# Sorting tokens to experts in a hybrid transformer kernel: where the rows are written, when, and in runs of how many

## The reference, cut to what matters

```
probs = softmax(t @ w_gate); tw, ti = top_k(probs, 2); tw = tw / sum(tw)
for e in range(8):
    we = sum(where(ti == e, tw, 0))
    h = gelu(t @ w1[e] + b1[e]) @ w2[e] + b2[e]      # 128 -> 512 -> 128
    out = out + we * h
```

## Time and profile before

| what | us |
|---|---|
| three runs | 902.31, 901.24, 893.77 (median 901.24) |
| the profiled execution, own time | 898.2 |
| its span, first to last instruction | 896.4 |
| PE busy | 767.0 (86%) |
| DVE, ACT, POOL busy | 544.5, 543.4, 484.2 |
| mean granted TensorE clock | 0.923 |

### The profile page before, as it was taken

How to read it: one execution, slowest core, us unless ns; L and a number is a source line. 1 busy time by engine, 2 the same in 40 slices (tenths; PEclk the granted TensorE clock), 3 DMA queues, 4 the chain that set the end, 5 groups by cost and what they waited for, 6 DMA issues and landing times.

```text
span 896.4 us, 21301 instructions
## 1 busy us (share of the span) xinstructions
PE 767.0 (86%) x7166; PEld 546.7 (61%) x7166; DVE 544.5 (61%) x1370; ACT 543.4 (61%) x1264; POOL 484.2 (54%) x906
## 2 busy tenths in 40 slices
PE   1999999999999399697988999999999948968970
PEld 1756655666565189497964565566666525958970
DVE  4699899788988123012486887878889822211232
ACT  0377777878787256154546676787877834715640
POOL 6667678747762621504645665844777273060436
PEclk9999999999999789698999899999999977978995
DMA  9300000000000436266210000000000042635842
GB/s 274 111 3 3 3 2 3 4 3 3 4 2 4 130 107 175 79 182 175 79 38 13 16 18 5 4 3 3 3 3 3 3 124 77 173 103 143 245 124 67
DMA packets 57657, 56.29 MB, mean 63 GB/s; under 512 B 6856, under 2 KB 42448, under 8 KB 57552
## 3 DMA queue, kind: packets, MB, share of 16 engines
q1 hardware_dynamic: 39200, 39.13, 15.5%
q0 software_dynamic: 4096, 8.40, 3.2%
q10 hardware_dynamic: 14256, 7.41, 2.9%
HBM read 40.10 MB, written 14.29 MB: 61 GB/s over the span
## 4 chain that ended last, share of the span: by engine, by line
PE 56%; DVE 21%; issue 11%; POOL 7%; DMA 3%; ACT 2%; another core or an unknown queue 0%; ACTq 0%; POOLq 0%; DVEq 0%; SPq 0%
DVE M L1109 11%; PE bankO L466 11%; PE bankR L720 8%; PE bankE L707 7%; PE bankE L485 7%; PE bankE L439 6%; DVE QKV L1071 2%; POOL Yg L1578 2%; PE bankR L452 2%; PE bankE L476 2%; PE bankR L506 2%; PE bankR L536 1%; PE bankR L738 1%; PE bankR L554 1%; DMA Yg<-sorted_y,SLOT 1%
## 5 line engine op out<-in xcount | busy, mean ns | idle before, releaser
L1109 DVE TENSOR_REDUCE M<-bankR 128x2 f32<-128x512 f32 x512 | 326.4, 684 | 62.7 <-PE bankR L452 56.9
L834 ACT ACTIVATE Pr<-bankE 128x512 f32<-128x512 f32 x512 | 277.7, 595 | 129.5 <-PE bankE L439 109.1
L466 PE MATMUL bankO<-Pr,Vx 128*32 128x256 f32 x2048 | 170.5, 406 | 18.8 <-issue 16.1
L452 PE MATMUL bankR<-KQ 32*128 32x256 f32 x1024 | 171.3, 339 | 5.0 <-DVE M L1109 2.9
L439 PEld LDWEIGHTS bankE<-KQ 32*128 32x128 f32 x1024 | 79.6, 188 | 97.1 <-issue 64.2
L439 PE MATMUL bankE<-KQ 32*128 32x256 f32 x1024 | 133.3, 335 | 0.5 <-issue 0.5
L1312 DVE COPY Yb<-bankR 128x128 f32<-128x128 f32 x92 | 26.4, 290 | 167.9 <-PE bankR L720 111.1
L452 PEld LDWEIGHTS bankR<-KQ 32*128 32x128 f32 x1024 | 110.1, 191 | 17.1 <-DVE M L1109 12.8
L951 ACT ACTIVATE G<-bankE,W 128x128 f32<-128x128 f32 x368 | 101.5, 384 | 24.8 <-PE bankE L707 14.0
L707 PE MATMUL bankE<-XTT,W 128*128 128x128 f32 x736 | 105.1, 288 | 11.4 <-issue 4.6
L1578 POOL DMA_INDIRECT Yg<-sorted_y,SLOT x64 | 62.2, 971 | 95.6 <-DMA sorted_y<-Yb 42.0
(11 more groups left out here) (169 smaller groups left out, 1147.0 us busy)
## 6 DMA issues: line engine op xcount, KB each, us to landing
W<-in_w1b SPq DMA_DIRECT2D x92, 258.0 KB
sorted_y<-Yb ACTq DMA_DIRECT2D x92, 64.0 KB
XT<-sorted_u SPq DMA_DIRECT2D x20, 256.0 KB
sorted_u<-Yg SPq DMA_DIRECT2D x2, 1472.0 KB, 9.7
KQ<-MT SPq DMA_DIRECT2D x128, 4.0 KB
X<-in_x SPq DMA_DIRECT2D x8, 128.0 KB, 7.3
sorted_u<-U,SLOT POOLq DMA_INDIRECT x64
Yg<-sorted_y,SLOT POOLq DMA_INDIRECT x64
```

Of the source, the lines that this page charges most:

```text
L452: k = mm(dve_bank("raw", layer, b, h)[:, z * T:z * T + T], QT[rows, kb, g, z * P:z * P + P], KT[rows, kb, g, :], start=True, stop=True)
L466: k = mm(bankO[SL * j:SL * j + SL, cols], Vx[:, b % VB, kc, HG * g + j, :], Pr[:, g % 2, j, kc, :], start=(g % 2 == 0 and kc == 0), stop=( ...
L834: nc.scalar.activation(Pr[:, (h // HG) % 2, h % HG], act_bank("S", layer, b, h).rearrange("p (k q) -> p k q", k=TT), ACT.Exp, scale=EXP_SC ...
L1109: v.tensor_reduce(M[:, b % 2, :, h], dve_bank("raw", layer, b, h).rearrange("p (t k) -> p t k", t=TT), AX.X, ALU.max, negate=True).then_in ...
```

## The change

`sorted_u` now has room for 1024 rows of every expert (CAP), so a row's place is expert x 1024 + rank, known without the other experts' counts. Blocks are therefore ranked one at a time: block 0 in steps 15 and 16, block 1 in step 17, block 2 around the prelude, block 3 at tiles 9 and 10. `sort_rows` becomes `place_rows` (per block, to SLOT_U), `sort_tiles` (per half: EID as before, and ROW, the first row of each tile) and `place_outputs` (per half: SLOT_Y for the gathers). The scatters go out in runs of four with other work or a wait between them. `load_x` loads one tile a DMA, its address read from ROW. Zeroing (now 8 MB) is 8 DMAs on ACT's queue in steps 4 to 11, from a POOL memset of G in step 2. `gather(0, 1)` is moved ahead of step 0.

```diff
+BG = GROUPS // 2
+CAP = HB * T
...
+        sorted_u = [nc.dram_tensor(f"sorted_u{k}", (E * CAP, D), F32).ap() for k in range(2)]
...
+        ranked = BlockEvent(sem("ranked"), 2)
+        placed = BlockEvent(sem("placed"), 5)
+        TILES_READY = 13
+        sorted_ = BlockEvent(sem("sorted"), TILES_READY + 5, 2)
...
+        def of_block(j):
+
+            return slice((j % 2) * BG * E, (j % 2) * BG * E + BG * E)
+
+        def ends_block(u, j):
+
+            return block_of(u) is not None and block_of(u)[1] == j
...
             sp.dma_start(sortc[:], d["sortc"]).then_inc(in_moe, 16)
-            sp.wait_ge(zero_set, 1)
-            for half in range(2):
-                sp.dma_start(sorted_u[half].rearrange("(i p) d -> p i d", p=P),
-                             Yg[:, 0:1, :].broadcast_to([P, NTL, D])).then_inc(zeroed, 16)
...
 
-            def load_x(ph, q):
-
-                half, i = divmod(GROUP[q][0], NTL)
-                n, k = GROUP[q][1], (ph * NGRP + q) % NXG
+            def load_x(ph, at):
+
+                half, i = divmod(at, NTL)
+                q, j = group_of(at)
+                k = (ph * NGRP + q) % NXG
+                r = sp.value_load(ROW[0:1, half, i:i + 1], min_val=0, max_val=E * CAP - P)
                 if i == 0:
                     sp.wait_ge(scattered[half], 16 * GROUPS * (ph + 1))
-                need(sp, x_turned, ph, q - NXG)
-                sp.dma_start(XT[:, k, 0:n, :],
-                             sorted_u[half][i * P:(i + n) * P, :].rearrange("(j p) d -> p j d", p=P)).then_inc(x_in[k], 16)
+                if j == 0:
+                    need(sp, x_turned, ph, q - NXG)
+                sp.dma_start(XT[:, k, j, :], sorted_u[half][bass.ds(r, P), :]).then_inc(x_in[k], 16)
...
                     load_w(ph, at)
-                for q in range(2 * NXG):
-                    load_x(ph, q)
+                for i in range(2 * NXG * XG):
+                    load_x(ph, i)
                 for at in range(NAT):
                     if at + NW < NAT:
                         load_w(ph, at + NW)
-                    if group_at(at - 1) is not None and group_at(at - 1) % (NGRP // 2) < NGRP // 2 - NXG:
-                        load_x(ph, group_at(at - 1) + NXG)
-                    if at == NTL - XG - 1:
-                        for q in range(NGRP // 2, NGRP // 2 + 2 * NXG):
-                            load_x(ph, q)
+                    if 2 * NXG * XG <= at + 11 < NTL:
+                        load_x(ph, at + 11)
+                    if NTL - XG <= at < NTL + XG:
+                        for i in range(2):
+                            load_x(ph, NTL + 2 * (at - NTL + XG) + i)
+                    if NTL + XG <= at < NAT - 3 * XG:
+                        load_x(ph, at + 3 * XG)
 
...
+                    do_totals(*block_of(gone))
+                if ends_block(gone, 1):
+                    do_rank(*block_of(gone))
+
+            def do_totals(ph, j):
+
+                need(pe, gated, ph, j)
+                ring_r.take(pe, ("totals", ph, j))
+                mm(dve_bank("totals", ph, j)[of_block(j), 0:P], OH[:, j * BT:j * BT + BT].rearrange("p n k e -> p (n k e)"),
+                   ones, start=True, stop=True).then_inc(ranked.sem, 1)
+                ring_r.give(("totals", ph, j), placed, ph, j, 1)
+
+            def do_rank(ph, j):
+
+
+                need(pe, placed, ph, j, 1)
+                ring_r.take(pe, ("rank", ph, j))
+                bank, n = dve_bank("rank", ph, j), BG * E
+                known = slice(0, n * (j % 2 + 1))
+                if j % 2:
+                    mm(bank[:, n:n + E], totals[:], of_expert, start=True, stop=True)
+                mm(bank[:, 0:n], below, OH[:, j * BT:j * BT + BT].rearrange("p n k e -> p (n k e)"), start=True, stop=False)
+                mm(bank[:, 0:n], totals[known, :], earlier_groups[known, of_block(j)], start=False,
+                   stop=True).then_inc(ranked.sem, 1)
+                if j % 2:
+                    ring_r.give(("rank", ph, j), sorted_, ph, j // 2, 1)
...
             def turn_x(ph, q):
                 x = ph * NGRP + q
-                pe.wait_ge(x_in[x % NXG], 16 * (x // NXG + 1))
+                pe.wait_ge(x_in[x % NXG], 16 * sum(GROUP[y % NGRP][1] for y in range(x % NXG, x + 1, NXG)))
...
+                if i == 0:
+                    do_rank(ph, 2)
                 if i == 9:
-                    do_rank(ph, 1, 0)
+                    do_totals(ph, 3)
                 if i == 10:
-                    do_rank(ph, 1, 1)
+                    do_rank(ph, 3)
                 if i in (12, 16):
                     do_weT(ph, i // 4 - 1)
...
+                do_totals(ph, 2)
                 do_wo(layer, NB - 1)
...
+            ZN = CAP * E * D // P // 4
+
+            def zero(half, x):
+
+                act.wait_ge(zero_set, 1)
+                act.dma_start(sorted_u[half].rearrange("(p i) d -> p (i d)", p=P)[:, x * ZN:x * ZN + ZN],
+                              G[:].rearrange("p n c r -> p (n c r)")[:, 0:ZN]).then_inc(zeroed, 16)
+
             for ph in range(2):
                 for s in own_steps(ph):
+                    if ph == 0 and 4 <= s < 12:
+                        zero((s - 4) // 4, s % 4)
                     step(*sequences(ph, s))
                 mixture(ph)
 
...
                 if m == (0, 0):
                     do_fold()
+                if ends_block(gone, 1):
+                    weigh(*block_of(gone))
...
                     rotate(*n, 2, 0)
                     rotate(*n, 2, 1)
...
                     norm3_in(*t)
+                if ends_block(gone, 0):
+                    copy_totals(*block_of(gone))
+                if ends_block(gone, 1):
+                    place_rows(*block_of(gone))
...
+            def copy_totals(ph, j):
+                need(dve, ranked, ph, j, 1)
+                v.tensor_copy(totals[of_block(j), :], dve_bank("totals", ph, j)[of_block(j), 0:P]).then_inc(placed.sem, 1)
+
+            def one_hot(first, n):
+
+                return OH[:, first // 2:(first + n) // 2].rearrange("p n k e -> p (n k) e")
+
+            def place_rows(ph, j):
+
+                half, at = j // 2, (j % 2) * BG
+                io = iota[:].unsqueeze(1).broadcast_to([P, BG, E])
+                need(dve, ranked, ph, j)
+                v.scalar_tensor_tensor(rank[:], io, float(CAP), dve_bank("rank", ph, j)[:, 0:BG * E].rearrange(
+                    "p (g e) -> p g e", e=E), ALU.mult, ALU.add).then_inc(placed.sem, 1)
+                need(dve, placed, ph, j, 2)
+                tt(rank[:], rank[:], one_hot(j * BG, BG), ALU.mult).then_inc(placed.sem, 1)
+                need(dve, placed, ph, j, 3)
+                v.tensor_reduce(place[:, at:at + BG], rank[:], AX.X, ALU.add).then_inc(placed.sem, 1)
+                need(dve, placed, ph, j, 4)
+                if ph:
+                    dve.wait_ge(scattered[half], 16 * GROUPS)
+                v.tensor_copy(SLOT_U[:, half, at:at + BG], place[:, at:at + BG]).then_inc(placed.sem, 1)
+                if j % 2:
+                    v.tensor_scalar(ntiles[:, 0], dve_bank("rank", ph, j)[:, BG * E:BG * E + E], 1.0 / P,
+                                    (P - 1) / (2.0 * P), ALU.mult, ALU.add).then_inc(sorted_.sem, 1)
+
+            def sort_tiles(ph, half):
...
+                v.tensor_scalar(spare[:], ntiles[:, 1], -float(P), float(CAP), ALU.mult, ALU.add).then_inc(sorted_.sem, 1)
+                tt(skip[:], past[:], spare[:].unsqueeze(1).broadcast_to([P, NTL, E]), ALU.mult).then_inc(sorted_.sem, 1)
+                v.tensor_reduce(row[:, 0], skip[:], AX.X, ALU.add).then_inc(sorted_.sem, 1)
+                v.scalar_tensor_tensor(row[:, 1], tile_no, float(P), row[:, 0], ALU.mult, ALU.add).then_inc(sorted_.sem, 1)
+                v.tensor_scalar(ROW[:, half], row[:, 1], float(E * CAP - P), None, ALU.min).then_inc(sorted_.sem, 1)
...
+            def place_outputs(ph, half):
+
+                def done(x):
+                    need(dve, sorted_, ph, half, TILES_READY + x)
+
+                done(-6)
+                v.scalar_tensor_tensor(move[:], iota[:], -float(CAP // P), first[:], ALU.mult, ALU.add).then_inc(sorted_.sem, 1)
+                done(1)
+                v.scalar_tensor_tensor(skip[:, 0:GROUPS], move[:].unsqueeze(1).broadcast_to([P, GROUPS, E]), float(P),
+                                       one_hot(half * GROUPS, GROUPS), ALU.mult, ALU.mult).then_inc(sorted_.sem, 1)
+                done(2)
+                v.tensor_reduce(moved[:, 0], skip[:, 0:GROUPS], AX.X, ALU.add).then_inc(sorted_.sem, 1)
+                done(3)
+                tt(moved[:, 1], moved[:, 0], place[:], ALU.add).then_inc(sorted_.sem, 1)
+                done(4)
+                v.tensor_copy(SLOT_Y[:, half], moved[:, 1]).then_inc(sorted_.sem, 1)
...
                 if i == 8:
                     weigh(ph, 3)
+                if i == 0:
+                    place_rows(ph, 2)
                 if i == 9:
```

(48 more changed lines are left out.)

100 lines of the change are left out of this document (40 added, 60 removed).

## The result

The changed kernel takes 904.32 us (median of 20 runs), the kernel before 898.1 us: ratio 1.0077, interval 1.0059 to 1.0096. The forecast was 863. The profiled execution spans 900.3 us against 896.4.

A forecast was written before the change was run, and what follows sets the result against it. PE bounds full attention steps, but all engines stall beside POOL's long scatter runs. Terms 9 + 11 + 9 + 9 + 2 - 3 - 1 = 36 off 898.2 gave 862, stated as 863 for the median; range 840 to 889.

The forecast's parts named there:

- The first four of a run are free: POOL's back-to-back scatters: the first four DMAs cost other engines nothing; from about the fifth on all engines crawl.
- Start of the mixture, 9 and 11 us: Step 18 to the first hidden layer: scatters in runs of four gain 9 us in phase 0, 11 in phase 1.
- Half boundary, 9 and 9 us: Mixture's first half to the second half's hidden layer: scatters in runs of four gain 9 us in each phase.
- The new wait: At each half boundary PE waits some 8 us for rows loaded tile by tile; 5 to 10 us expected in the profile.
- S + 49: When PE finishes half 0's outputs, about 49 us after the first hidden layer, whose time S is 323.31 in the old profile.
- Ranking, 3 us: Per-block ranking in nearly full steps 15 to 17 costs about 1.5 us a phase, 3 us in all, bounds 0 to 6.
- Gather 2 us: Second gather issued ahead of the norm, at 406 instead of 415.71, removes a PE wait: gain 2 us.
- zeroing 1 us: POOL's larger memset of G in step 2 shows as about 1 us of cost; the 8 MB of writes cost nothing.
- its stated loss case: Gather moved ahead of the norm: a loss of 4 us if eight gathers in a row crawl like scatters do.
- Rival 3: SP's row loads at start and boundary become the bound: gain gone at 2.05 us a load, 909 at 2.3; chance 0.07.
- Rival 2: Pauses between scatter runs too short, a crawl with every second run, half 1 gains nothing: 888; chance 0.12.
- Rival 4: Stall comes with weight loads and writes together, whatever the scatters' grouping; only the start gains: 888 or 890; chance 0.07.

The follow-up runs named there:

- Both edits: Changed kernel with row addresses read early, the boundary's row loads issued earlier, and block 1 ranked in step 18; with runs of four, 0.9891 of the kernel before on chip 1.

## Why the prediction was wrong

*The first four of a run are free: the step that failed.* "The first four DMAs of a run cost other engines nothing" was read from PE, which was covered by released work. Lateness beside a run: two at most 1.2 us, four 1.6 to 3.7, eight 7.4 + 1.3; beside sixteen DVE takes two tiles in the 21 us from 355.6 to 376.6. Four runs of four cost less than one of sixteen, but not nothing: half 0 takes 53.5 and 54.2 us with them, 61.7 and 61.1 with sixteen in a row, and 46.1 without a stall. So 7 to 8 us a phase of what the prediction gave back stayed lost in the mixture, and the eight gathers held up tile 26 on top. This is the first of three steps that failed; the other two are the price of the ranking and SP's order of loads.

*Start of the mixture, 9 and 11 us.* The scatters of block 0 did go in steps 16 and 17. In step 18 I had the second run follow at once; it waited 5.41 us for its score, since PE was slow: I had priced step 18 at full clock. It took 20.7 us, 8.9 less than before, and steps 16 and 17 took 7.7 more, so the move of the scatters bought nothing: the first hidden layer came at 324.31 instead of 313 to 315, later even than before.

*Half boundary, 9 and 9 us.* The new wait was rightly foreseen (5.9 us of PE waits, forecast 5 to 10, and SP's 1.1 us a load). What failed is the middle: half 0's outputs ended at S + 60, not S + 49. Some 8 us of this are the stall beside the runs of four and the clock lost with it (0.93); the rest was a count too low, since even without a stall the outputs end at S + 52 to S + 53. The boundary's rows were also late for a reason I had in hand and took as given: SP's order put them behind weight loads that wait for a buffer. The other order, with addresses read early, is worth about 8 us a boundary beside runs of four on chip 8, and 6.3 and 7.7 on chip 1 (there with the ranking moved too).

*Ranking, 3 us.* Sizes right, price wrong. I counted 1.3 us of DVE and took 1.5 us a phase, bounded by 6 in all. Moving only block 1's ranking out of step 17 took 17 us out of steps 17 and 18 on a chip without the stall, and 9 on chip 1. I had written that steps 15 to 17 are nearly full; I had not followed which bank the gate's matmul takes, nor the clock: with runs of two on chip 8 the granted clock falls to 1.2 GHz at 284.5, 0.4 us behind the end of PE's wait of 1.8 us, and stays there for 27.3 us in which PE is always busy.

*Gather 2 us, zeroing 1 us.* The gather measured nothing; its stated loss case, eight in a row crawling, is what cancelled the gain. The start became 1.4 us shorter instead of 1 longer, which is within what executions differ by.

*The rivals.* Rival 3 (SP's queue the bound, slower) came nearest: the sign is right and loads from fixed places gave 39 us. But its condition, a load slower than 1.1 us, was not met; 1.1 us was enough, since the loads stood one behind another, and behind weights. Rival 2 named pauses too short; it is true that a crawl comes with every run, pause or not. Rival 4 (the length of a run does not matter) fails where the stall is: four in a row delay a tile by 3.0 us, eight by 7.4. On the two chips without it length doesn't matter either, but there is nothing to stall, so that isn't the rival's case. The Trainium skill, "SBUF — State Buffer", section "Who interferes with whom", says that DMA never contends with a compute engine. With runs of eight on chip 10 the trace agrees (0.03 us late). On chip 1 engines are held up beside the same runs (7.35 us late); whether by contention for memory or by something else no run here shows.

*The account.* Forecast and measurement lie 41 us apart. Both edits gave 27 us (chip 1), and runs of two 9 in the mixture by the stretches, 15 by the ratios (across chips 1 and 4). From the changed kernel to the one with all three it is 30 us if the result's 904.3 is set against 874.5, and 43 through chip 1's ratio. So the three steps account for 30 to 43 of the 41 us; the shares are no firmer than that. That the changed kernel came out close to the one before is chance: a gain of 7 to 8 us in each half 0 stood against losses of about the same size at the boundaries and in step 17, which have other causes.

The version that beats both kernels is the one with both edits and runs of two: 0.9726 of the kernel before where the stall is, and level with it (0.9981, interval 0.9955 to 1.0007) where it isn't. The change's gain is thus a cure for a stall that not every chip has. One cost remains in all versions that load row by row: phase 1's half 1 takes 42 to 44 us instead of 39.0. In its first tiles SP spends 3.3 us on a weight load and two row loads while PE needs 1.8 us a tile; that this is the cause was not tried by itself.

## What to carry to other kernels

When one engine's burst holds up others, measure the harm on the consumer that waits most often, not on the engine with work queued; compare the end of each producer with the start of its consumer. When work is moved into a full step, follow the banks and the clock: a wait of 1 to 2 us on PE can cost several more at half clock in the next step. Loads should not queue behind a load that waits for a buffer; reading a load's address ahead of its wait helps only if the queue has time to spare there, as it had not at the start of the mixture. A wait that is meant to split a burst has to be checked in the trace: several here were met before they were reached. And a gain that rests on a stall should be measured on more than one chip.

## What the runs showed of the hardware that I had not expected

- The stall beside back-to-back indirect DMAs from POOL is there on chips 1, 4 and 6 and absent on 8 and 10, with the same program: 897 to 899 us against 860 to 862 for the kernel before. Within a chip every trace agreed, and one program (both edits, runs of two) had tile 26 late by 6.5 us on chip 4 and on time on chip 8. Why chips differ stays open, and so does what carries the stall. Plain DMAs from POOL's queue ran only where nothing stalls, so whether they are harmless elsewhere wasn't tried.
- Where it exists it begins at about the third DMA (2.7 us into the run) and holds for both directions, scatters and gathers. A run of two still makes an evacuation up to 1.2 us late.
- A row load with an address from a table takes SP 1.1 us, of which 0.49 remain when the address is already read (3.94 us for eight).
- PE can be busy through 20.1 of 20.1 us at 1.2 GHz (granted clock 0.50), behind a step 17 in which it waited 1.8 and 0.5 us for DVE. Without those two waits step 17 keeps clock 1.00, and step 18 (with block 1's ranking in it) takes 18.2 us at clock 0.63 in one phase and 14.0 at 0.88 in the other.
